# Triangular inverse of a gated delta-rule layer: two matmul levels and a Newton step are replaced by a VectorE level, one float32 level and a substitution

## The chip, the cores and the metric

The kernel runs on one core of a Trainium2 chip. The metric is the device time of one execution in microseconds. The core has five engines with an instruction queue each, all in order: TensorE (PE), VectorE (DVE), ScalarE (ACT), GpSimd (POOL), and SyncE (SP), which here only waits on semaphores and issues DMAs.

## The reference

One layer on x of 2 x 2048 tokens by 256 features. The attention part is a gated delta rule with 8 key heads and 16 value heads of 128 x 128 state:

```python
mixed = silu(causal_conv4(layernorm(x) @ Wqkv.T + bqkv))   # q, k (8 heads), v (16 heads)
beta, g = sigmoid(x @ Wb.T + bb), -exp(A_log) * softplus(x @ Wa.T + ba + dt_bias)
def step(state, (q_t, k_t, v_t, g_t, b_t)):                # for each token, each head
    state = state * exp(g_t)
    delta = (v_t - k_t @ state) * b_t
    state = state + outer(k_t, delta)
    return state, q_t @ state
core = rmsnorm(outs) * norm_w * silu(x @ Wz.T + bz)
x = x + layernorm(core @ Wout.T + bout)
x = x + layernorm(shared_ffn(h) + top8_of_16_experts(h))   # h = layernorm(x)
```

## The kernel before

The tokens are cut into 32 chunks of 128. Inside a chunk the recurrence is a linear system: with the strictly lower triangular 128 x 128 matrix L of each head (decayed products of keys), delta = (I + L)^-1 (...). The kernel builds the inverse explicitly, then solves with a matmul. The 16 heads go in 4 groups of 4, and one pass of the software pipeline, an *item*, is one group of one chunk: 128 items, and each engine's queue is written out by hand in its own `item` function. In item w several groups are at work: a = w+3 (projection and convolution), f = w+2 (keys, decays, L), v = w+1 (merging of the inverse), w itself (state and output), and the feed-forward part of the chunk before.

The inverse of group f takes this road. POOL writes minus L (`minus_l`, L1484). SP writes it to DRAM (`triangle_out`, L408, tensor DL), and reads back the eight 16 x 16 diagonal blocks of each of the 4 heads as 32 lanes of 256 numbers (`blocks_in`, L412, tile Cb). POOL inverts them by doubling, 22 instructions that each wait for the one before, and turns the result (`base_inverse`, L1583 to L1607, tile Yb). SP writes block inverses and their transposes to DRAM (`inverses_out`, L417, DX), waits until they have landed and reads them as 128 x 128 matrices (`inverses_in`, L424 and L425, tiles XiT and Xi). Then come three merging levels on TensorE in float32r (`invert_q` L547, `invert_xt` L560, `invert_x` L570), each with a mask on DVE (`mask_q`, L1194) and PSUM copies on ACT (L937, L944), and a Newton step (`turned`, `residual`, `correct`; L577, L584, L586, L593) that ends in the copy to Tt (`refined`, L1210). The state part of item w (`ks_qs`, `solve`, `az`, `new_state`) uses Tt in two halves of two heads.

In SP's item the order is: Xf of the next chunk, Xr of this one (in one item of four each), then `triangle_out(f)`, `blocks_in(f)`, `inverses_out(f)`, `inverses_in(f)`, and the store of the chunk. So SP issues 6 DMAs in an item, and 3 more per chunk.

Of the kernel before, what the change touches and what calls it, by code (L numbers as in the profile page):

```python
# [33 lines left out]
F32R = mybir.dt.float32r  # L34
# [5 lines left out]
P = 128  # L40
# [5 lines left out]
GK = HK // GROUPS  # L46
TILES = 2 * GK + GH
TAPS = 4
LO = 4
LEVELS = 7 - LO  # L50
SLOTS = 8
BASE = 1 << LO
BLOCKS = P // BASE
LANES = BLOCKS * GH
HSTRIDE = P * P + P
# [11 lines left out]
C_KEEP = C_LEVEL + LEVELS * P  # L67


def constants(chunks, chunks_of_batch):  # L70
# [8 lines left out]
    for n in range(LEVELS):  # L79
        b = r >> (LO + n)  # L80
        f[:, C_LEVEL + n * P:C_LEVEL + (n + 1) * P] = (b[:, None] % 2 == 1) & (b[None, :] == b[:, None] - 1)
    f[:, C_LEVEL:C_LEVEL + P] += np.eye(P)
# [19 lines left out]
def layer_kernel(nc, x, wqkv, conv, wz, wba, rows, cols, wout, shared1, wlat, shared2, wup, rw, rw2,  # L102
# [6 lines left out]
    with ctx:  # L109
# [22 lines left out]
        IdR = sb("IdR", [P, GH, P], F32R)  # L132
        NegR = sb("NegR", [P, P], F32R)
# [35 lines left out]
        Vs = sb("Vs", [P, GROUPS, GH, P])  # L169
        Kn = sb("Kn", [P, GROUPS, GK, P])  # L170
        AT = sb("AT", [P, GROUPS, GH, P])
# [13 lines left out]
        Ln = sb("Ln", [P, 2, GH, P])  # L185
        LnR = sb("LnR", [P, GH, P], F32R)


        Xi = sb("Xi", [P, GH, P], F32R)
        XiT = sb("XiT", [P, GH, P], F32R)  # L190
        Qi = sb("Qi", [P, GH, P], F32R)
# [4 lines left out]
        Yb = sb("Yb", [LANES, 2, BASE * BASE], F32R)  # L196
        Tp = sb("Tp", [LANES, BASE ** 3 // 8])
        Tm = sb("Tm", [LANES, BASE * BASE // 4])
        DL = nc.dram_tensor("DL", (GH * HSTRIDE,), F32, kind="Internal").ap()
# [9 lines left out]
        def blocks_of(part):  # L209
            return scratch(part, [[BASE * (P + 1), LANES], [P, BASE], [1, BASE]])  # L210
# [6 lines left out]
        Z = sb("Z", [P, 2, P])  # L217
        O = sb("O", [P, GH, P])
# [27 lines left out]
        def heads(bank):  # L246
# [3 lines left out]
        BASE_STEPS = 2 + sum(2 * (3 if n == 1 else BASE // (2 << n) + n) for n in range(1, LO))  # L250
# [3 lines left out]
            q_full=LEVELS + 1, xt_full=LEVELS, x_full=LEVELS - 1, xr_full=1, c_full=1,  # L254
            ks_full=2, qs_full=2, zs_full=2, az_full=2, ds_full=2, coT_full=1, po_full=1,

            y_done=2, silu_done=2, gz_done=1, zb_done=1, lnk_done=1, rki_done=1, sc_done=1, partsT_done=1, ex_done=1,
            kn_done=1, vs_done=1, xi_done=LEVELS, qg_done=2, z_done=2, lnf_done=1, fr_done=1, coT_done=1,
            xt_done=LEVELS, sq_done=1, lnr_done=1, oq_done=1,

            bk_done=1, tails_done=2, convqk_done=TAPS, convv_done=TAPS, sse_done=1, epq_done=1, kkq_done=1, hg_done=4, parts_done=5,
            q_done=LEVELS + 1, tt_done=1, r_done=2, o_done=2, s_done=2, so_done=1, vv_done=1, core_done=1, acc_done=1,
# [3 lines left out]
            ln_out=16, lc_in=16, xs_out=32, xs_seen=1, xb_in=32,  # L266
# [34 lines left out]

        def ahead(w, n):

            t, g = w
            return t + (g + n) // GROUPS, (g + n) % GROUPS

        def run(eng, item):
# [6 lines left out]
            steps = next(n for n in (30, 6, 5, 3, 2, 1) if (chunks - 2) % n == 0)  # L314
            with eng.Fori(0, (chunks - 2) // steps) as i:
                for k in range(steps):
                    for g in range(GROUPS):
                        item((i * steps + k + 1, g), "cafispe")
# [57 lines left out]
        def _(sp):  # L376
# [29 lines left out]
            def triangle_out(f):  # L406
                sp.wait_ge(sem["neg_done"], at("neg_done", f))
                sp.dma_start(rows_of(DL), Ln[:, f[1] % 2, :, :]).then_inc(sem["ln_out"], 16)  # L408

            def blocks_in(f):  # L410
                sp.wait_ge(sem["ln_out"], at("ln_out", f))
                sp.dma_start(Cb[:, :].rearrange("p (i j) -> p i j", i=BASE), blocks_of(DL)).then_inc(sem["lc_in"], 16)  # L412

            def inverses_out(f):
                sp.wait_ge(sem["base_done"], at("base_done", f))
                for n in range(2):
                    sp.dma_start(blocks_of(DX[n]), Yb[:, n, :].bitcast(F32).rearrange("p (i j) -> p i j", i=BASE))\  # L417
                        .then_inc(sem["xs_out"], 16)

            def inverses_in(f):  # L420
                sp.wait_ge(sem["xs_out"], at("xs_out", f))
                sp.sem_inc(sem["xs_seen"], 1)
                sp.wait_ge(sem["c_full"], at("c_full", ahead(f, -1)))
                sp.dma_start(XiT[:, :, :].bitcast(F32), rows_of(DX[1])).then_inc(sem["xb_in"], 16)  # L424
                sp.dma_start(Xi[:, :, :].bitcast(F32), rows_of(DX[0])).then_inc(sem["xb_in"], 16)  # L425

            def item(w, stages):
                t, g = w
                f = ahead(w, 2)
# [17 lines left out]
            run(sp, item)  # L447
# [4 lines left out]
        def _(pe):  # L452
# [45 lines left out]
            def ss(f):  # L498
                pe.wait_ge(sem["xt_done"], at("xt_done", ahead(f, -2)))
# [17 lines left out]
            def vtr(f):  # L517
                pe.wait_ge(sem["tt_done"], at("tt_done", ahead(f, -2)))
# [15 lines left out]
            def invert_q(v, n, front=None):  # L534
                if n == 0:
                    if front:
                        pe.wait_ge(sem["ex_done"], at("ex_done", ahead(v, 1)))
                    else:
                        pe.wait_ge(sem["q_done"], at("q_done", ahead(v, -1)))
                    pe.wait_ge(sem["xb_in"], at("xb_in", v))  # L540
                    mm(bQ[:, :], identb, identb.unsqueeze(1).to_broadcast([P, GH, P]), start=True, stop=True)
                    pe.wait_ge(sem["lnr_done"], at("lnr_done", v))
                else:
                    pe.wait_ge(sem["xt_done"], at("xt_done", v, n))
                    pe.wait_ge(sem["q_done"], at("q_done", v, n))
                for h in range(GH):
                    last = mm(heads(bQ)[:, h, :], LnR[:, h, :], XiT[:, h, :], start=(n > 0), stop=True,  # L547
                                  skip_group_check=True)
                last.then_inc(sem["q_full"], 1)

            def invert_xt(v, n, front=None):
                if n == 0 and front:
                    pe.wait_ge(sem["partsT_done"], at("partsT_done", ahead(v, 1)))
                elif n == 0:
                    pe.wait_ge(sem["xt_done"], at("xt_done", ahead(v, -1)))
                pe.wait_ge(sem["q_done"], at("q_done", v, n + 1))
                if n:
                    pe.wait_ge(sem["xi_done"], at("xi_done", v, n))
                for h in range(GH):
                    last = mm(heads(bXT)[:, h, :], Xi[:, h, :], Qi[:, h, :], start=(n == 0 and h == 0), stop=True,  # L560
                              skip_group_check=True)
                last.then_inc(sem["xt_full"], 1)

            def invert_x(v, n, front=None):
                if n == 0 and front:
                    pe.wait_ge(sem["vs_done"], at("vs_done", ahead(v, 1)))
                elif n == 0:
                    pe.wait_ge(sem["tt_done"], at("tt_done", ahead(v, -1)))
                for h in range(GH):
                    last = mm(heads(bX)[:, h, :], Qi[:, h, :], Xi[:, h, :], start=(n == 0 and h == 0), stop=True,  # L570
                                  skip_group_check=True)
                last.then_inc(sem["x_full"], 1)

            def turned(v):
                pe.wait_ge(sem["xt_done"], at("xt_done", v))
                for h in range(GH):
                    last = mm(heads(bX)[:, h, :], XiT[:, h, :], IdR[:, 0, :], start=(h == 0), stop=True, skip_group_check=True)  # L577
                last.then_inc(sem["xr_full"], 1)

            def residual(v):  # L580
                g = v[1]
                pe.wait_ge(sem["neg_done"], at("neg_done", v))
                for h in range(GH):
                    mm(heads(bQ)[:, h, :], Ln[:, g % 2, h, :], XiT[:, h, :].bitcast(F32), start=(h == 0), stop=False,  # L584
                       skip_group_check=True)
                mm(bQ[:, :], NegR[:, :], XiT[:, :, :], start=False, stop=True, skip_group_check=True)\  # L586
                    .then_inc(sem["q_full"], 1)

            def correct(v):
                pe.wait_ge(sem["xi_done"], at("xi_done", v))  # L590
                pe.wait_ge(sem["q_done"], at("q_done", v))
# [1089 lines left out]
```

## Time and profile before

| | |
|---|---|
| median of 3 runs | 3363.12 us (3360.05 to 3366.53) |
| profiled execution, first to last instruction | 3361.6 us |
| TensorE busy | 3184.6 us, 95% |
| VectorE / ScalarE / GpSimd busy | 2731.3 / 2411.1 / 2147.3 us |
| mean granted TensorE clock | 0.989 |

The profiled execution's own time is not listed apart from its span; the span is 1.5 us under the median of the runs. Busy times are sums over instructions. A matmul's end is modelled and overlaps the next one, so that the spacing of starts, not the duration, tells what a matmul costs. A float32 matmul is two records in the trace.

### The profile page before, as it was taken

The numbers are of one execution on the slowest core, as the hardware profiler recorded it, in microseconds if no ns is written. First come the engines' busy times: TensorE is split into PE (matmuls) and PEld (weight loads), VectorE is DVE, ScalarE is ACT, GpSimd is POOL, SyncE is SP. The second block draws the span as 40 slices with busy tenths as digits, with TensorE's granted clock in tenths as the row PEclk, the third lists the DMA queues.
The fourth block names the chain that finished last, engine by engine and source line by source line (L and its number), as shares of the span: only waits on it lengthen the run. The fifth ranks groups of instructions, "written<-read, shape, count | busy, mean of one in ns | idle before, by whom it ended". The sixth has DMA issues, their size and how long they took to land.

```text
span 3361.6 us, 77100 instructions
## 1 busy us (share of the span) xinstructions
PE 3184.6 (95%) x23968; PEld 2828.4 (84%) x23968; DVE 2731.3 (81%) x8720; ACT 2411.1 (72%) x5922; POOL 2147.3 (64%) x5380
## 2 busy tenths in 40 slices
PE   4999999999999999999999999999999999999996
PEld 3888888888888888888888888888888888888885
DVE  4788888888888888888888888888888888888874
ACT  3777777777777777777777777777777777777762
POOL 3766666666666666666666666666666666666660
PEclk8999999999999999999999999999999999999997
DMA  4111111111111111111111111111111111111110
GB/s 182 43 40 38 44 40 35 45 41 38 39 45 35 39 47 38 36 45 38 38 45 41 36 37 46 38 39 47 37 35 45 41 38 42 43 35 39 47 36 11
DMA packets 424113, 144.75 MB, mean 43 GB/s; under 512 B 211168, under 2 KB 421664, under 8 KB 423200
## 3 DMA queue, kind: packets, MB, share of 16 engines
q1 hardware_dynamic: 423712, 139.83, 15.9%
q8 instruction: 200, 3.28, 0.4%
q14 instruction: 201, 1.65, 0.2%
HBM read 93.11 MB, written 46.66 MB: 42 GB/s over the span
## 4 chain that ended last, share of the span: by engine, by line
PE 66%; ACT 14%; DVE 5%; issue 5%; POOL 5%; DMA 4%; SPq 0%; ACTq 0%; DVEq 0%; POOLq 0%
PE bF L474 8%; PE bB L648 6%; PE bQ L547 5%; ACT L850 4%; PE bXT L560 4%; PE bB L733 3%; PE bB L720 3%; PE bS L615 3%; PE bD L630 3%; PE bS L623 3%; PE bF L485 3%; PE bS L607 3%; PE bF L487 3%; PE bD L608 2%; PE bX L570 2%
## 5 line engine op out<-in xcount | busy, mean ns | idle before, releaser
L1151 DVE SCALAR_TENSOR_TENSOR Y<-bF,Cv,Y 128x127 f32<-128x127 f32 (+2 forms) x3072 | 852.2, 339 | 8.3 <-ACT Y L867 3.4
L474 PE MATMUL bF<-XnT,Wqkv 128*128 128x128 f32 x4096 | 530.9, 277 | 0.5 <-ACT XnT L986 0.5
L474 PEld LDWEIGHTS bF<-XnT,Wqkv 128*128 128x128 f32 x4096 | 504.4, 193 | 9.3 <-issue 1.8
L867 ACT ACTIVATE Y<-bF,Cv 128x128 f32<-128x128 f32 x1024 | 383.4, 455 | 102.5 <-PE bF L474 102.5
L937 ACT ACTIVATE XiT<-bXT 128x512 fp32r<-128x512 f32 x384 | 229.0, 596 | 298.0 <-PE bXT L560 293.4
L1590 POOL TENSOR_TENSOR Tp<-Tp 32x64 f32<-32x64 f32 (+2 forms) x768 | 362.1, 472 | 60.2
L1194 DVE TENSOR_TENSOR Qi<-bQ,Cf 128x512 fp32r<-128x512 f32 x384 | 262.8, 684 | 98.1 <-PE bQ L547 97.0
L850 ACT ACT_TABLE_LOAD x257 | 329.7, 1283 | 5.4 <-PEq L1674 0.7
L560 PEld LDWEIGHTS bXT<-Qi,Xi 128*128 128x128 f32 x1536 | 221.8, 191 | 118.0 <-issue 88.8
L560 PE MATMUL bXT<-Qi,Xi 128*128 128x128 f32 x1536 | 298.7, 317 | 14.3 <-DVE Qi L1194 2.5
L1583 POOL TENSOR_TENSOR Tp<-Yb,Tm 32x64 f32<-32x64 f32 (+1 forms) x384 | 276.0, 719 | 30.1
L1583 POOL TENSOR_TENSOR Tp<-Cb,Yb 32x64 f32<-32x64 f32 (+1 forms) x384 | 274.6, 715 | 30.1
L1598 POOL TENSOR_TENSOR Yb<-Cb,Cf 32x8 fp32r<-32x8 f32 x128 | 25.9, 202 | 402.1 <-DMA Cb<-DL 402.1
L547 PE MATMUL bQ<-XiT,LnR 128*128 128x128 f32 x1536 | 264.2, 295 | 19.6 <-ACT XiT L937 19.5
L547 PEld LDWEIGHTS bQ<-XiT,LnR 128*128 128x128 f32 x1536 | 211.6, 191 | 41.1 <-ACT XiT L937 29.1
L648 PE MATMUL bB<-Wout,CoT 128*128 128x256 f32 x1024 | 244.2, 382 | 0.9 <-ACT CoT L973 0.8
L1484 POOL TENSOR_TENSOR Ln<-Ex,KKQ 128x512 f32<-128x512 f32 x128 | 163.1, 1274 | 125.6 <-issue 121.7
L944 ACT ACTIVATE Xi<-bX 128x512 fp32r<-128x512 f32 x384 | 228.4, 595 | 3.6 <-PE bX L577 2.3
L1517 POOL TENSOR_TENSOR HG<-LnbG,Lnk 128x4 f32<-128x4 f32 x128 | 29.2, 228 | 295.5 <-ACT Lnk L900 295.4
L648 PEld LDWEIGHTS bB<-Wout,CoT 128*128 128x128 f32 x1024 | 185.9, 192 | 21.6 <-ACT CoT L973 1.2
L615 PE MATMUL bS<-R,Tt 128*128 128x128 f32 x1024 | 165.9, 285 | 9.9 <-DVE Tt L1210 9.9
L1020 ACT ACTIVATE Rl<-bB 128x512 f32<-128x512 f32 x124 | 74.1, 597 | 139.0 <-PE bF L721 139.0
(234 smaller groups left out, 9269.8 us busy)
## 6 DMA issues: line engine op xcount, KB each, us to landing
DL<-Ln SPq DMA_DIRECT2D x128, 256.0 KB, 2.2
XiT<-DX SPq DMA_DIRECT2D x128, 256.0 KB, 2.8
Xi<-DX SPq DMA_DIRECT2D x128, 256.0 KB, 3.2
DX<-Yb SPq DMA_DIRECT2D x256, 32.0 KB, 1.9
Xf<-x SPq DMA_DIRECT2D x32, 128.0 KB, 3.1
Wqkv<-wqkv SPq DMA_DIRECT2D x4, 1024.0 KB, 17.0
Cb<-DL SPq DMA_DIRECT2D x128, 32.0 KB, 1.9
Xr<-x SPq DMA_DIRECT2D x32, 128.0 KB, 3.3
```

Source lines behind the costliest of these rows:

```text
L474: last = mm(bank[:, i, :], Wqkv[:, k, c:c + P], XnT[:, k, :], start=(k == 0), stop=(k == KT - 1))
L547: last = mm(heads(bQ)[:, h, :], LnR[:, h, :], XiT[:, h, :], start=(n > 0), stop=True, skip_group_check=True)
L560: last = mm(heads(bXT)[:, h, :], Xi[:, h, :], Qi[:, h, :], start=(n == 0 and h == 0), stop=True, skip_group_check=True)
L615: last = mm(heads(bS)[:, i, :], Tt[:, 2 * p + i, :], R[:, i, :], start=True, stop=True)
L648: last = mm(bB[:, 0:HID], CoT[:, h, :], Wout[:, g * GH + h, :], start=(h == 0), stop=(h == GH - 1))
L850: nc.scalar.add_instruction(mybir.InstLoadActFuncSet(name=nc.get_next_instruction_name(), act_func_set_id=TABLES[name], engine=mybir.Engin ...
L867: last = op(Y[:, tile, :], bank[:, i, :], ACT.Identity, scale=c[:, TAPS - 1:TAPS], bias=c[:, TAPS:TAPS + 1])
L937: op(XiT[:, :, :], heads(bXT), ACT.Copy).then_inc(sem["xt_done"], 1)
L1151: last = stt(y, bank[:, i, 0:P - shift], Cv[:, g * TILES + tile, n:n + 1], y, ALU.mult, ALU.add)
L1194: tt(Qi[:, :, :], heads(bQ), level, ALU.mult).then_inc(sem["q_done"], 1)
L1583: then(tt(view(Tp[:, :], p * m ** 3, [[m * m, m], [m, m], [1, m]]), pair(left, p), pair(right, p), ALU.mult))
L1590: then(tt(lo, lo, hi, ALU.add))
```

## The change

Of the 128 x 128 inverse only the two 64 x 64 diagonal halves are built. The doubling on POOL to 16 x 16 blocks stays, with the same instructions and sizes, but is cut in two: the steps of width 1, 2 and 4 for f in item w, the last step (width 8) for v at the start of the next item, and the turning late in that item. Level 16 to 32 goes to DVE, on 128 lanes of 2 rows (`wide`, 5 instructions). Level 32 to 64 is one float32 level on TensorE (`merge_q`, `mask_q`, `merge_x`) with one addition on DVE (`merged`). The last level is never formed: the solve becomes a substitution (`solve_halves`, `solve_cross`, `solve_rest`) with two ACT copies of 64 rows (`upper_half`, `crossed`). The Newton step and its identities go. Tiles Vs, Kn, AT and Ln become rings of three, Yb is doubled.

The DVE level needs its operands on other lanes, and this is done by DMAs of 16 partitions. SP's new functions and its order:

```diff
+            def cross_in(f):
+                sp.wait_ge(sem["wide_done"], at("wide_done", ahead(f, -1)))
+                for n in range(SPREAD):                      # SPREAD = 8
+                    sp.dma_start(Cm[n * PAIRS:(n + 1) * PAIRS, :]..., blocks_of(DL, 0, BASE)).then_inc(sem["cm_in"], 16)
+            def inverses_spread(v):
+                sp.wait_ge(sem["base_done"], at("base_done", v, BASE_STEPS - 1))
+                sp.wait_ge(sem["wide_done"], at("wide_done", ahead(v, -1)))
+                for n in range(SPREAD):
+                    sp.dma_start(Ya[n * PAIRS:(n + 1) * PAIRS, :], Yb[0:PAIRS, ...]).then_inc(sem["ya_in"], 16)
+                for n in range(SPREAD):
+                    sp.dma_start(Yc[n * PAIRS:(n + 1) * PAIRS, :], Yb[PAIRS:LANES, ...]).then_inc(sem["yc_in"], 16)
+            def crosses_out(v):
+                sp.wait_ge(sem["wide_done"], at("wide_done", v))
+                for n in range(SPREAD):
+                    sp.dma_start(rows_in_blocks(DX[0], ..., ROWS_OF, BASE), Yu[...]).then_inc(sem["xu_out"], 16)
+                    sp.dma_start(rows_in_blocks(DX[1], ..., BASE, ROWS_OF), Yv[...]).then_inc(sem["xv_out"], 16)
...
+                if "i" in stages:
+                    inverses_spread(v)
+                if "f" in stages:
+                    triangle_out(f)
                 if g == 1 and "s" in stages:
                     tokens_in(t)
+                if "i" in stages:
+                    inverses_out(v)                          # 4 DMAs, waits for the turning
+                    crosses_out(v)
                 if "f" in stages:
-                    triangle_out(f)
                     blocks_in(f)                             # 2 DMAs instead of 1
-                    inverses_out(f)
-                    inverses_in(f)
+                if "i" in stages:
+                    inverses_in(v)                           # waits for xs_out, xu_out, xv_out
+                if "f" in stages:
+                    cross_in(f)
```

The DVE level, and POOL's new order:

```diff
+            def wide(v):
+                dve.wait_ge(sem["cm_in"], at("cm_in", v))
+                dve.wait_ge(sem["ya_in"], at("ya_in", v))
+                tt(terms, across(Ya), down(Cm), ALU.mult)            # 128 x 512
+                nc.vector.tensor_reduce(Tr, summed, AX.X, ALU.add)   # 128 x 32 <- 128 x 512
+                dve.wait_ge(sem["yc_in"], at("yc_in", v))
+                tt(terms, across(Tr), down(Yc), ALU.mult)            # 128 x 512
+                nc.vector.tensor_reduce(Yu, summed, AX.X, ALU.add)
+                nc.vector.tensor_copy(Yv, Yu turned)                 # 128 x 32
...
 POOL item:
+  base_terms(v,3,0) base_halved(v,3,0,0) exponents(f) base_halved(v,3,0,1) base_joined(v,3,0) base_terms(v,3,1)
+  edge_terms(a) base_halved(v,3,1,0) base_halved(v,3,1,1) key_exponents(f) base_joined(v,3,1)
+  edge_sum(a,0) exponent_part/rest(f,0) edge_sum(a,1) exponent_part/rest(f,1) exponent_part(f,2)
+  decay_keys(w,0) minus_l(f) attention(f) base_turned(v) decay_keys(w,1)
+  base_ones(f) end_exponents(f) base_terms/halved/joined(f,1..2)
```

TensorE's merging and solve, and the masks:

```diff
-   invert_q x3, invert_xt x3, invert_x x2, turned, residual, correct, solve
+   merge_q(v):       mm(bQ[h], Ln[ring(v), h], XiT[h])            # 4 x float32
+   merge_x(w):       mm(bX[h], Qi[h], Xi[h])                      # 4 x float32, early in the next item
+   solve_halves(w,p) mm(bS[i], Tt, R)  -> ACT upper_half (64 rows of Ym)
+   solve_cross(w,p)  mm(bX[..], Ln, Ym) -> ACT crossed (64 rows of Wm)
+   solve_rest(w,p)   mm(bS[i], Tt, Wm), added in PSUM
-   DVE: mask_q x4, refined (copy)      ACT: inverse_t x3, inverse x3, rounded_l
+   DVE: mask_q x1, merged (addition)   ACT: upper_half x2, crossed x2
```

All five queues are put into a new order. On DVE `wide(v)` stands after `update_o(w, 0)` and ahead of `right_side(w, 1)`; on TensorE `merge_q(v)` is nearly the last step of the item and `merge_x` the third of the next; `update_s(w, 1)` is DVE's last. Masks, norms and sums stay on the engines they are on.

## Rows read from the trace of the kernel before

**Rows 1.** The page: busy time of each engine, and TensorE's granted clock in 40 slices.
```profile
PE 3184.6 (95%) x23968; PEld 2828.4 (84%) x23968; DVE 2731.3 (81%) x8720; ACT 2411.1 (72%) x5922; POOL 2147.3 (64%) x5380
PEclk8999999999999999999999999999999999999997
```

**Rows 2.** Busy time by stretch, from the first to the last issue of Cb.
```profile
53.20:3269.30 3216.10, 3102.80 (x23438) 2759.33 (x23438) 2662.42 (x8516) 2364.32 (x5813) 2128.19 (x5327) 1.00 0.16 40
```

**Rows 3.** The chain of waits, one stretch: start, us, what, records.
```profile
1610.54 0.89 PE bF L474 x8
...
1613.03 0.45 PE bS L623 x4
...
1614.81 0.21 PE bQ L541
1615.03 0.40 PE bQ L547 x4
...
1616.47 0.65 PE bXT L560 x4
```

**Rows 4.** Groups of instructions by shape, DVE and ACT: busy us, mean ns.
```profile
L1194 DVE TENSOR_TENSOR Qi<-bQ,Cf 128x512 fp32r<-128x512 f32 x384 | 262.8, 684 | 98.1 <-PE bQ L547 97.0
L937 ACT ACTIVATE XiT<-bXT 128x512 fp32r<-128x512 f32 x384 | 229.0, 596 | 298.0 <-PE bXT L560 293.4
L956 ACT ACTIVATE Z<-bS 128x256 f32<-128x256 f32 x256 | 102.2, 399 | 19.3 <-PE bS L615 19.3
L1210 DVE COPY Tt<-bX 128x512 f32<-128x512 f32 x128 | 88.4, 690 | 6.4 <-PE bX L593 3.0
L1240 DVE TENSOR_REDUCE Ss<-CoT 128x4 f32<-128x512 f32 x128 | 86.0, 672 | 0.0
L1157 DVE TENSOR_SCALAR Bk<-Cv,Cf 128x8 f32<-128x8 f32 x128 | 29.2, 228 | 0.0
```

**Rows 5.** SP's DMA issues in order of time: start us, us, instruction.
```profile
1606.26 0.85 SPq L417 DMA_DIRECT2D DX<-Yb  x2
1608.58 0.38 SPq L424 DMA_DIRECT2D XiT<-DX  x1
1609.00 0.51 SPq L425 DMA_DIRECT2D Xi<-DX  x1
1609.55 0.50 SPq L404 DMA_DIRECT2D out<-Yo  x1
1610.10 0.43 SPq L400 DMA_DIRECT2D Xf<-x  x1
1615.28 0.37 SPq L408 DMA_DIRECT2D DL<-Ln  x1
1617.46 0.32 SPq L412 DMA_DIRECT2D Cb<-DL  x1
```

**Rows 6.** One line of the kernel: duration of each issue of DX (ns).
```profile
L417 SPq DMA_DIRECT2D DX<-Yb x256: 303/321/1230, 67.3 to 3283.8; - x128
```

**Rows 7.** The page: DMA issues, KB each, median us to landing; queue's packets.
```profile
Xi<-DX SPq DMA_DIRECT2D x128, 256.0 KB, 3.2
DX<-Yb SPq DMA_DIRECT2D x256, 32.0 KB, 1.9
Cb<-DL SPq DMA_DIRECT2D x128, 32.0 KB, 1.9
q1 hardware_dynamic: 423712, 139.83, 15.9%
```

**Rows 8.** Waits, SP's queue and POOL: us in total, times, longest.
```profile
SPq L417 <- POOL Yb L1607: 1797.1, 128, 15.1
POOL Yb L1598 <- DMA Cb<-DL: 402.1, 128, 4.7
```

**Rows 9.** POOL in order of time, one item: start us, us, instruction.
```profile
1609.16 0.20 POOL L1517 TENSOR_TENSOR HG<-LnbG,Lnk 128x4 f32<-128x4 f32 x1 [2.62 <-ACT Lnk L900]
...
1610.90 0.23 POOL L1498 TENSOR_TENSOR Hd<-Tails,Cv 128x24 f32<-128x24 f32 x1
...
1615.21 1.26 POOL L1484 TENSOR_TENSOR AT<-Ex,KKQ 128x512 f32<-128x512 f32 x1
1619.40 0.20 POOL L1598 TENSOR_TENSOR Yb<-Cb,Cf 32x8 fp32r<-32x8 f32 x1 [2.92 <-DMA Cb<-DL]
...
1630.55 0.29 POOL L1592 TENSOR_TENSOR Yb<-Tp 32x64 fp32r<-32x64 f32 x1
1630.91 0.72 POOL L1607 TENSOR_TENSOR Yb<-Yb,Cf 32x256 fp32r<-32x256 f32 x1
```

More of the change, by code:

```diff
@@ L305, in ahead, with run @@
             return t + (g + n) // GROUPS, (g + n) % GROUPS
-        def run(eng, item):
+        def run(item):
             for g in range(GROUPS):
@@ L313, in run @@
                 item((0, g), "cafis" + "p" * (g > 0))
[L314 to L318, printed above, removed]
+            for t in range(1, chunks - 1):
+                for g in range(GROUPS):
+                    item((t, g), "cafispe")
             for g in range(GROUPS):
@@ L414, in inverses_out @@
-            def inverses_out(f):
-                sp.wait_ge(sem["base_done"], at("base_done", f))
                 for n in range(2):
[L417 to L425, printed above, removed]
+                    sp.dma_start(Cb[n * PAIRS:(n + 1) * PAIRS, :].rearrange("p (i j) -> p i j", i=BASE),
+                                 blocks_of(DL, n * BASE, n * BASE)).then_inc(sem["lc_in"], 16)
@@ new lines, in inverses_out @@
+            def inverses_out(v):
+                sp.wait_ge(sem["base_done"], at("base_done", v))
+                sp.wait_ge(sem["xb_in"], at("xb_in", ahead(v, -1)))
+                for n in range(2):
+                    for half in range(2):
+                        sp.dma_start(blocks_of(DX[n], half * BASE, half * BASE),
+                                     Yb[half * PAIRS:(half + 1) * PAIRS, v[1] % 2, n, :].rearrange("p (i j) -> p i j", i=BASE))\
+                            .then_inc(sem["xs_out"], 16)
@@ L446, in _ @@
             sp.wait_ge(cleared, 32)
-            run(sp, item)
+            run(item)
             sp.wait_ge(stored, 16 * (chunks + 1))
@@ L564, in invert_x @@
[L564 to L571, printed above, removed]
-                last.then_inc(sem["x_full"], 1)
@@ L574, in turned @@
[L574 to L587, printed above, removed]
@@ L614, in solve, with solve_cross, solve_rest @@
                 for i in range(2):
-                    last = mm(heads(bS)[:, i, :], Tt[:, 2 * p + i, :], R[:, i, :], start=True, stop=True)
+                    last = mm(heads(bS)[:, i, :], Tt[:, 2 * p + i, :], R[:, i, :], start=(i == 0), stop=False,
+                              skip_group_check=True)
+                last.then_inc(sem["ys_full"], 1)
+            def solve_cross(w, p, front):
+                t, g = w
+                pe.wait_ge(sem["ym_done"], at("ym_done", w, p + 1))
+                if p == 1 and front:
+                    pe.wait_ge(sem["vs_done"], at("vs_done", ahead(w, 2)))
+                for i in range(2):
+                    last = mm(heads(bX)[:, 2 * p + i, :], Ln[:, ring(w), 2 * p + i, :], Ym[:, i, :], start=True, stop=True)
+                last.then_inc(sem["ws_full"], 1)
+            def solve_rest(w, p):
+                t, g = w
+                pe.wait_ge(sem["wv_done"], at("wv_done", w, p + 1))
+                for i in range(2):
+                    last = mm(heads(bS)[:, i, :], Tt[:, 2 * p + i, :], Wm[:, i, :], start=False, stop=True,
+                              skip_group_check=True)
                 last.then_inc(sem["zs_full"], 1)
@@ L840, in _ @@
             pe.wait_ge(early, 16 * len(EARLY))
-            run(pe, item)
+            run(item)
         @block.scalar
@@ L1469, in item @@
                     experts(t - 1, "result", 0)
+                if invert:
+                    mask_q(v)
+                if state:
+                    out_norm(w)
                 if c and g == 0:
                     chunk_front(t + 1, "ba")
-            run(dve, item)
+                if state:
+                    update_s(w, 1)
+            run(item)
         @block.gpsimd
@@ new lines, in base_halved, with base_joined @@
+            def base_halved(f, n, side, k):
+                m, pairs, left, right, into = operands(f, n, side)
+                width = m >> (k + 1)
+                base_wait(f, base_steps(n, side) + terms_of(n) + k)
+                lo = view(Tp[:, :], 0, [[m, pairs * m * m], [1, width]])
+                hi = view(Tp[:, :], width, [[m, pairs * m * m], [1, width]])
+                tt(lo, lo, hi, ALU.add).then_inc(sem["base_done"], 1)
+            def base_joined(f, n, side):
+                m, pairs, left, right, into = operands(f, n, side)
+                base_wait(f, base_steps(n, side) + terms_of(n) + n - 1)
+                if m == 2:
+                    halves = [view(Tp[:, :], k * 4 * pairs, [[4, pairs], [2, 2], [1, 2]]) for k in range(2)]
+                else:
+                    halves = [view(Tp[:, :], k, [[m ** 3, pairs], [m * m, m], [m, m]]) for k in range(2)]
+                tt(into, halves[0], halves[1], ALU.add).then_inc(sem["base_done"], 1)
@@ L1614, in item @@
                 new, front, invert, state, post, e, c = [s in stages for s in "afispec"]
+                if invert:
+                    base_terms(v, 3, 0)
+                    base_halved(v, 3, 0, 0)
                 if front:
                     exponents(f)
+                if invert:
+                    base_halved(v, 3, 0, 1)
+                    base_joined(v, 3, 0)
+                    base_terms(v, 3, 1)
                 if new:
[L1618 removed]
+                    edge_terms(a)
+                if invert:
+                    base_halved(v, 3, 1, 0)
+                    base_halved(v, 3, 1, 1)
+                if front:
+                    key_exponents(f)
+                if invert:
+                    base_joined(v, 3, 1)
+                if new:
+                    edge_sum(a, 0)
+                if front:
+                    exponent_part(f, 0)
+                    exponent_rest(f, 0)
+                if new:
+                    edge_sum(a, 1)
+                if front:
+                    exponent_part(f, 1)
+                    exponent_rest(f, 1)
+                    exponent_part(f, 2)
                 if state:
[L1620 removed]
+                    decay_keys(w, 0)
                 if front:
@@ L1623, in item @@
                     attention(f)
-                    base_inverse(f)
-            run(pool, item)
+                if invert:
+                    base_turned(v)
+                if state:
+                    decay_keys(w, 1)
+                if front:
+                    base_ones(f)
+                    end_exponents(f)
+                    base_terms(f, 1, 0)
+                    base_joined(f, 1, 0)
+                    base_terms(f, 1, 1)
+                    base_joined(f, 1, 1)
+                    base_terms(f, 2, 0)
+                    base_halved(f, 2, 0, 0)
+                    base_joined(f, 2, 0)
+                    base_terms(f, 2, 1)
+                    base_halved(f, 2, 1, 0)
+                    base_joined(f, 2, 1)
+            run(item)
 def kernel(**inputs):
```

632 lines of the change are left out of this document (316 added, 316 removed).

## The prediction

> **What bounds the kernel now.** I read the page first: TensorE is busy 95% of the span at a granted clock of 1.00 in all but the outermost slices, VectorE 81%, the others less [rows 1]. Then the stretch from the first to the last issue of Cb, which is 127 items: 3216.1 / 127 = 25.32 us an item, of which TensorE is busy 24.4, VectorE 21.0, ScalarE 18.6 and GpSimd 16.8 [rows 2]. The rest of the span, 3361.6 - 3216.1 = 145.5 us, is ramp. So TensorE's queue sets the pace, and an edit counts there first. Then the transfers: SP issues few and waits long, 1797 us in all for the block inverses (14 us of every item), and GpSimd waits 402 us (3.1 us an item) for Cb [rows 8]. These waits cost nothing today, because the inverse is made an item ahead. The reader should keep the roles in mind: before, SP is idle most of an item.
>
> **What the change takes off and puts on the engines, per item.** TensorE: a float32 matmul of 128 columns costs 0.22 us (four in 0.89, two in 0.45); four float32r ones cost 0.40 to 0.65 us, I take 0.5 [rows 3]. Removed are 40 float32r matmuls (3+3+2+1+1 groups of four: 10 x 0.5 = 5.0), four float32 (0.9), a bf16 identity of 512 columns (0.21) and a float32r one, bounded by 0.2 and 0.9, taken as 0.3: 6.4 us. Added are merge_q, merge_x, solve_cross and solve_rest, 4 float32 each: 16 x 0.22 = 3.6 us. Net -2.8 us. VectorE: three masks of 0.684 go (-2.05); the copy to Tt at 0.690 becomes an addition of the same size, taken equal. `wide` is two products of 128x512 and two reductions of 128x512, nearest rows 0.684 and 0.672, and a copy of 32 columns, between 0.2 and 0.7 (I take 0.2): 2.9 us. Net +0.9, so 21.9 us [rows 4]. ScalarE loses seven copies of 0.6 and gains four of 64 rows by 256, at most 0.4 each by the row of Z, at least nothing: -2.6 to -4.2. GpSimd keeps its instructions. If engines alone counted, TensorE's item would be 25.3 - 2.8 = 22.5 us.
>
> **What it does to the queue of SP.** Transfers per item: `inverses_spread` 16, `triangle_out` 1, `inverses_out` 4, `crosses_out` 16, `blocks_in` 2, `inverses_in` 2, `cross_in` 8: 49 where there were 6. Every issue occupies SP. The shortest of 256 issues of DX lasts 303 ns [rows 6]; in a burst the starts stand 0.42 to 0.55 us apart, and the pair for DX takes 0.85 us [rows 5]. Size hardly matters in these rows: 32 KB in 0.32, 256 KB in 0.37 to 0.51. No row shows an issue of 16 partitions. The new transfers leave in bursts of 8 and 16, so the nearest row is the pair: i = 0.85 / 2 = 0.425 us each. The low end is 0.30, the high end 0.55 (the longest spacing in these rows). A cost below 0.30 is no end of this range; it is the rival below.
>
> 49 x 0.425 = 20.8 us of issuing would still fit into an item. What does not fit is that most of it has become serial with GpSimd. SP's order puts `blocks_in(f)` behind `crosses_out(v)`, and the group f of this item is the v of the next. The circle, starting when GpSimd has joined the last block of v:
>
> 1. 16 spreads; the last begins after 15 i and lands 1.9 us later [rows 7]. The landing of a transfer inside SBUF is not shown; I take that of Cb and DX.
> 2. `wide` can do its first two instructions before Yc is there, but product, reduction and turning come after: 0.68 + 0.67 + 0.2 = 1.6 us [rows 4].
> 3. `crosses_out` waits for this. 16 issues, then the two of Cb, the last of which begins after 17 i and lands after 1.9 us.
> 4. GpSimd waits for Cb and doubles. Today the 22 steps from L1598 to the last L1592 take from 1619.40 to 1630.84, 11.4 us [rows 9]. The same steps, in the same sizes, with about seven small instructions set between them (exponents, edge_terms, key_exponents, end_exponents, at 0.2 each, some in today's gaps), are 12.6 us. They end in the join that starts the next circle.
>
> Sum: 32 i + 1.9 + 1.6 + 1.9 + 12.6 = 32 i + 18.0. With i = 0.425 it is 31.6 us an item, against 22.5 that TensorE would need. It is equal to today's 25.3 at i = 0.23.
>
> Other edits are hidden in this circle. The 4 issues of `inverses_out` and the one of DL lie between the spread and the landing of Yc plus `wide` (5 i = 2.1 against 1.9 + 1.6), unless the turning is late: after the join come the parts, decay_keys, minus_l, attention and the turning, by today's rows 7.3 us from L1517 to the end of attention with 0.6 for the edge terms and 0.6 for the second decay_keys to be taken off, and 0.7 for the turning, 6.8 in all; the spread takes 16 i = 6.8. So it is covered at 0.425 and decides only for small i. `inverses_in` and `cross_in` (10 i, and the landing of Yv) fall beside GpSimd's 12.6 us. A second circle goes through TensorE: join, spread, wide (15 i + 3.5), 16 crosses and their landing (15 i + 1.9), XiT and Xi (i + 3.2), merge_q 0.9, mask 0.7, then in the next item merge_x 0.9, ss 0.9, proj 0.9, kkq 0.9, the halves and qs 0.9, ScalarE's Qg and Ln 0.9, key_exponents and the join 0.6: 31 i + 16.2 = 29.4 us. It is 2 us under the first, so TensorE waits but does not add. On VectorE, `wide` waits in front of `right_side(w, 1)`, the second taps and `update_s`: all of this stands still until Yc has landed, and TensorE with it; their work after the wait is some 10 us and has room in 31.6.
>
> The 64-byte and 8-byte rows of Cm and Yv bring the packets from 3310 an item to some 7900 (Cm 2048, Yv 2048, Yu 256, Ya and Yc 256). The queue's packets take 15.9% of 16 engines now, 20 ns each [rows 7]. At that mean a Yv transfer keeps its 16 engines 0.32 us, less than one issue; I count nothing. At twice the mean it would be 0.64 and the eight would add 1.7 us an item, 220 us, which is inside my range.
>
> Sum for the run: 127 x 31.6 = 4013, and the ramps unchanged at 145.5: a span of 4159 us. Runs lie 1.5 us over the span before, so 4160 us.
>
> **A rule of the skill against this.** The shortest issue in this trace is 303 ns [rows 6]. The Trainium skill (DMA: Bandwidth & Descriptors, Anatomy of one DMA) puts the sequencer's dispatch of one DMA at about 50 ns and calls descriptor generation small; it describes GpSimd's path. The trace disagrees sixfold for SP. With 0.05 and the 0.04 us that stand between two issues, i = 0.09, the change would be a gain, as follows.
>
> **The rivals.** *B, cheap small issues (faster).* An issue of 16 partitions might cost much less than one of 32 or 128. The mechanism decides at i = 0.23. Under it the first circle falls behind another: join to turning 6.8, then 4 + 16 + 2 issues, landing 1.9, GpSimd 12.6: 21.3 + 22 i. At i = 0.09 that is 23.3 us, over TensorE's 22.5 and VectorE's 21.9: 127 x 23.3 + 145.5 = 3105 us. For it: no row has this shape, and cost varies a little with shape. Against: seven forms of transfers between 32 KB and 256 KB in this stretch all lie at 0.32 or above [rows 5]. 0.12.
>
> *C, TensorE loses its clock, or bursts jam (far slower).* TensorE's work would be 21.6 us of a 31.6 us item, with its idle time in one piece in front of `right_side(w, 1)`. The granted clock is below 1.00 only in the first and last slices, where it idled [rows 1]. At the lower of its two levels, 1.2 for 2.4 GHz, all of its work would take 43 us and the run over 5600; with a third of the work at that level it takes 29 us and stays hidden. Bursts at 0.55 us give 35.6 us an item, 4670 us. What lies beyond 4640: 0.06.
>
> *D, no change in time.* The circle might be looser than I read it and end near 25.3 by chance: 3360 us, 0.02. That the engines' own work becomes the bound is excluded, none grows by more than 0.9 us.
>
> **How the numbers follow.** Forecast 0.80, B 0.12, C 0.06, D 0.02. A measurement of this kernel tells 0.2% (7 us) from no change. i = 0.30 gives 27.6 us and 3650 us, 0.55 gives 4670; the range is 3610 to 4640, which leaves out B, C and D. Since nearly all of the chance has one sign, this is the forecast's own range too. Faster 0.12, same 0.02, slower 0.86.
>
> **What would show it.** Issues of Cb some 31.6 us apart; 16 issues of Ya and Yc in about 6.8 us; VectorE idle before the second product of `wide` for Yc, GpSimd idle before L1598's successor for Cb, longer than 3.1 us an item; TensorE busy near 70%. Wrong would be: issues of 16 partitions under 0.23 us, or Cb issued before the crosses are out, or TensorE idle for something else than VectorE's queue.

## The result, and the profile after

The changed kernel takes 4850.0 us (median of 4 runs, 4846.7 to 4854.0), the kernel before 3362.1 us beside it: 1.442 times as long, 95% interval 1.440 to 1.444. The direction was forecast, the size was not: 4160 us were forecast, and the time lies 210 us over the upper end of the range.

The page of the changed kernel, busy time and granted clock [rows 1]:

```profile
PE 3353.3 (69%) x21664; PEld 2860.1 (59%) x21664; DVE 3106.5 (64%) x8976; ACT 2178.7 (45%) x5538; POOL 2175.1 (45%) x5380
PEclk7888889888888888888888898888888888888887
```

No engine is busy 70% of the span any more, and the granted clock has fallen from 0.99 to 0.86 of 2.4 GHz. The chain that ended last, by engine and by line, from the same page:

```profile
SPq 44%; POOL 28%; DMA 10%; issue 10%; DVE 5%; PE 1%; POOLq 0%; ACT 0%; DVEq 0%; ACTq 0%
SPq L451 13%; POOL Tp L1644 11%; SPq L453 11%; SPq L468 10%; SPq L470 9%; POOL Tp L1653 7%; DMA Cb<-DL 5%; DMA Yc<-Yb 5%; DVE Tq L1230 3%; POOL Tp L1640 2%; POOL Yb L1662 2%; POOL Tm L1662 2%; DVE Yu L1233 2%; SPq L437 1%; POOL Hd L1537 1%
```

TensorE, 95% busy before, is on 1% of this chain. SP's queue, which does nothing but issue DMAs, is on 44% of it, GpSimd on 28%, landings on 10%. One turn of the chain, in order of time (start us, us, what), is the circle of the prediction:

```profile
2429.01 0.52 SPq L451
2429.57 0.62 SPq L451
...
2434.24 0.58 SPq L453
...
2438.02 0.59 SPq L453
2438.65 1.84 DMA Yc<-Yb
2440.59 1.03 DVE Tq L1230
2441.64 0.70 DVE Yu L1233
2442.57 0.30 SPq L468
2442.91 0.42 SPq L470
...
2447.69 1.66 SPq L470
...
2451.32 0.45 SPq L437
2451.81 1.88 DMA Cb<-DL
...
2458.30 1.48 POOL Tp L1644
...
2465.01 1.20 issue
2466.71 0.52 SPq L451
```

L451 and L453 are the 16 spreads (9.6 us from the first to the start of the last, which is not on a line of its own: its landing is counted from there), then Yc lands, VectorE finishes `wide`, L468 and L470 are the 16 crosses (8.7 us), L437 the two reads of Cb, then GpSimd's doubling up to the next spread. This turn is 2466.71 - 2429.01 = 37.7 us. Over the run the issues of Cb span 55.3 to 4741.4 us, 36.9 us an item where it was 25.3 [rows 2], and 159 us are ramp. The waits (us in total, times, longest) that answer to those of before [rows 8]:

```profile
POOL Yb L1623 <- DMA Cb<-DL: 1909.0, 128, 17.1
PE bS L635 <- DVE R L1258: 962.2, 127, 9.6
DVE Tq L1230 <- DMA Yc<-Yb: 389.5, 128, 4.1
SPq L451 <- POOL Yb L1662: 1039.3, 128, 11.5
POOL HG L1559 <- ACT Lnk L933: 141.2, 79, 8.7
```

GpSimd waits 14.9 us of each item for Cb, where it was 3.1; TensorE waits 7.5 us for the right side that stands behind `wide` in VectorE's queue. The durations of single issues in ns (shortest, median, longest), to set beside [rows 6]:

```profile
L451 SPq DMA_DIRECT2D Ya<-Yb x1024: 507/589/1836, 69.5 to 4758.6; - x171
L468 SPq DMA_DIRECT2D DX<-Yu x1024: 302/448/1832, 82.9 to 4774.4; - x171
L470 SPq DMA_DIRECT2D DX<-Yv x1024: 302/423/1827, 83.3 to 4774.9; - x171
L443 SPq DMA_DIRECT2D Cm<-DL x1024: 303/448/1560, 56.2 to 4746.7; - x171
```

Here is the largest mis-sized term: a transfer from 16 partitions to 16 others (2 KB for Ya, and 16 KB for Yc with the same median) holds SP for 0.59 us. No transfer of the kernel before went from SBUF to SBUF, and the longest median of its transfers inside an item was 0.51 us.

### The profile page after: what moved, and what is told of

Same layout as the page of the kernel before. It is cut to its first block, busy times and chain, and to the rows that moved or that the text cites. A ratio compares the mean times of both kernels' runs of the same rounds, so it can differ in the third digit from the quotient of the medians.

```text
span 4844.9 us, 78493 instructions
## 1 busy us (share of the span) xinstructions
PE 3353.3 (69%) x21664; PEld 2860.1 (59%) x21664; DVE 3106.5 (64%) x8976; ACT 2178.7 (45%) x5538; POOL 2175.1 (45%) x5380
## 3 DMA queue, kind: packets, MB, share of 16 engines
q1 hardware_dynamic: 1101600, 179.90, 19.8%
q14 instruction: 250, 2.05, 0.1%
## 4 chain that ended last, share of the span: by engine, by line
SPq 44%; POOL 28%; DMA 10%; issue 10%; DVE 5%; PE 1%; POOLq 0%; ACT 0%; DVEq 0%; ACTq 0%
SPq L451 13%; POOL Tp L1644 11%; SPq L453 11%; SPq L468 10%; SPq L470 9%; POOL Tp L1653 7%; DMA Cb<-DL 5%; DMA Yc<-Yb 5%; DVE Tq L1230 3%; POOL Tp L1640 2%; POOL Yb L1662 2%; POOL Tm L1662 2%; DVE Yu L1233 2%; SPq L437 1%; POOL Hd L1537 1%
## 5 line engine op out<-in xcount | busy, mean ns | idle before, releaser
L635 PEld LDWEIGHTS bS<-R,Tt 128*128 128x128 f32 x1024 | 197.7, 260 | 995.3 <-issue 979.9
L965 ACT ACTIVATE Ym<-bS 64x256 f32<-64x256 f32 x256 | 96.4, 377 | 1036.6 <-PE bS L635 1036.6
L1230 DVE TENSOR_TENSOR Tq<-Tr,Yc 128x512 f32<-128x512 f32 x128 | 130.2, 1018 | 389.5 <-DMA Yc<-Yb 389.5
L1225 DVE TENSOR_TENSOR Tq<-Ya,Cm 128x512 f32<-128x512 f32 x128 | 175.9, 1374 | 310.5 <-DMA Ya<-Yb 310.5
L1267 DVE TENSOR_TENSOR O<-Qg,bS 128x256 f32<-128x256 f32 x256 | 107.8, 421 | 372.5 <-ACT Qg L976 349.3
L686 PE MATMUL bB<-Wout,CoT 128*128 128x256 f32 x1024 | 339.8, 492 | 0.8 <-ACT CoT L998 0.8
L668 PEld LDWEIGHTS bD<-Z,Kd 128*128 128x128 f32 x1024 | 196.0, 264 | 213.9 <-issue 212.1
L668 PE MATMUL bD<-Z,Kd 128*128 128x128 f32 x1024 | 223.0, 358 | 137.5 <-ACT Qg L976 137.5
L686 PEld LDWEIGHTS bB<-Wout,CoT 128*128 128x128 f32 x1024 | 266.5, 275 | 46.8 <-ACT CoT L998 1.1
L1275 DVE SCALAR_TENSOR_TENSOR S<-S,Sc,bD 128x128 f32<-128x128 f32 x512 | 153.9, 341 | 149.6 <-PE bD L668 149.6
```

Source lines behind the costliest of these rows:

```text
L635: last = mm(heads(bS)[:, i, :], Tt[:, 2 * p + i, :], R[:, i, :], start=(i == 0), stop=False, skip_group_check=True)
L668: last = mm(heads(bD)[:, i, :], Kd[:, p, i, :], Z[:, i, :], start=True, stop=True)
L686: last = mm(bB[:, 0:HID], CoT[:, h, :], Wout[:, g * GH + h, :], start=(h == 0), stop=(h == GH - 1))
```

## The experiments

The theory is the circle through SP. Its rivals: the clock, the engine work of the new design, the total of issuing or of packets, and a second circle that was underrated. The runs on the changed kernel are medians of two executions, those on the kernel before of four.

### How much of the loss is the issues

All five families of eight DMAs cut to one each, with otherwise the same queues:

```diff
-  cm_in=16 * SPREAD, ya_in=16 * SPREAD, yc_in=16 * SPREAD, xu_out=16 * SPREAD, xv_out=16 * SPREAD
+  cm_in=16, ya_in=16, yc_in=16, xu_out=16, xv_out=16
-                for n in range(SPREAD):      # in cross_in, inverses_spread (twice), crosses_out
+                for n in range(1):
```

> Each of the five families of eight DMAs (Ya, Yc, Yu, Yv, Cm) is cut to its first one: 14 issues an item instead of 49. Seven eighths of the lanes are left unmoved (zeros), so the output is not the reference's; every engine instruction stays. Theory (the circle through SP): the issues leave it and what is left runs over the turning: join to turning 7.1 us, 4 + 2 + 2 issues at 0.47, landing 1.9, GpSimd 12.6 = 25.4 us an item, 3390 us, and the granted clock of TensorE back near 1.0. Rival (the new DVE level, the substitution and the new queue order are slow by themselves, or the clock does it): stays above 4400.

Measured: 3669.5 us, ratio 1.091 (1.086 to 1.096). The 35 issues, with what they move, are 1181 of the 1488 us that the change costs. The granted clock is back at 0.944 with nothing changed but these transfers, so most of its fall was a consequence. The time is not 3390, because the chain has moved to VectorE (40%) and TensorE (33%); 306 us over the kernel before remain.

### Which issues

Only Ya and Yc cut to one:

> Only Ya and Yc are cut to one DMA each (left unmoved lanes are zeros, so the output is not the reference's). Theory: 14 issues of 0.65 us leave the circle, 9.1 us, but the turning then decides (7.1 us after the join): 7.1 + 20 issues x 0.48 + 2 x 0.47 + 1.9 + 12.6 = 32.2 us an item, 4240 us. Rival (all issues cost the same 0.425 us, and the excess over the forecast is something else, such as the clock): 14 x 0.425 = 6 us off, 31 us an item or 4090, with the spacing of Ya at 0.42.

Measured: 4538.8 us, 300 us over the theory's figure. The removal of 9 us of issues brought 2.4 us an item. The turning decides as expected (SP waits 267 us for it and 555 us for minus L), but the way to it does not lead over GpSimd's doubling, as the figure had it. The chain of this run goes from Cb's landing over two small steps of GpSimd and ScalarE's Qg into TensorE's queue, and from there to minus L, the masked attention (AT), the turning and the crosses. TensorE is on 34% of it, SP's queue on 26%.

Only Yu and Yv cut to one:

> Only Yu and Yv are cut to one DMA each (the rest of the cross blocks stays zero, so the output is not the reference's). Theory: 14 issues of 0.48 us leave the circle: 36.9 - 6.7 = 30.2 us an item, 3990 us. Rival (the small rows of 8 and 64 bytes jam the DMA engines, and the issues only queue up behind them): more than that, since 2048 of 8600 packets go, and the spacing of the Ya issues falls under 0.6.

Measured: 4491.8 us, 500 us over. Spacing of the Ya issues is still 0.63 us, so that no jam behind small rows is what makes them long. What took over is in its waits:

```profile
POOL HG L1559 <- ACT Lnk L933: 695.8, 127, 8.5
```

That is 5.5 us an item, where it was 1.1 with all the crosses. L1559 is key_exponents, which stands just before the join. Lnk comes from ScalarE, behind Qg, behind TensorE's next item: the second circle, which the prediction put 2 us under the first.

Only Cm cut to one:

> Only Cm is cut to one DMA (the rest of the lanes are zeros, so the output is not the reference's). Theory: these issues stand beside GpSimd's doubling and are not on the circle: no change, 4850 within 30 us. Rivals: SP's total issuing time is the bound, then 7 x 0.49 = 3.4 us an item go, 4410 us; or the number of packets is, then more.

Measured: 4841.6 us, against 4850.0: no change. 896 issues and 229 thousand packets less bring nothing, because they stand where SP waits anyway: its wait for the join grows from 1039 us in all to 1378. Neither the total of issuing nor the number of packets is the bound.

### The second circle

SP's reads of Cb ahead of the writes:

```diff
+                if "f" in stages:
+                    blocks_in(f)
                 if "i" in stages:
                     inverses_out(v)
                     crosses_out(v)
-                if "f" in stages:
-                    blocks_in(f)
```

> One reordering of SP: the reads of Cb go ahead of the writes of the block inverses and of the crosses. One-circle theory (only spread, wide, crosses, Cb, doubling counts, as forecast): 16 x 0.63 + 0.53 + 2.3 for DL to land + 0.95 + 1.9 + 12.6 = 28.4 us an item, 3770 us. Two-circle theory (the way over XiT, merge_q, Qg, Ln and key_exponents back to the join is as long, 37 us): SP now also waits for DL to land ahead of the crosses, so 37.4 + 2.3 = 39.7 us an item, 5200 us.

Measured: 5164.0 us, as the theory of two circles had it (5200) and far from 3770. From the chain of this run (start us, us, what) and its waits:

```profile
2402.07 2.33 DMA DL<-Ln
2404.42 0.32 SPq L437
2404.79 1.89 DMA Cb<-DL
...
2417.87 15.20 issue
2433.10 0.20 POOL HG L1559
```

```profile
POOL HG L1559 <- ACT Lnk L933: 1605.5, 127, 15.2
POOL Yb L1623 <- DMA Cb<-DL: 844.3, 128, 8.6
```

GpSimd now has Cb early, has done everything up to key_exponents by 2417.9, and stands 15.2 us for Lnk (the wait is on its line in the second block; the chain calls it issue). The first circle is cut, and the second is longer by the 2.3 us of DL's landing.

The same, with the second circle cut as well:

```diff
+                if invert:
+                    base_joined(v, 3, 1)
                 if front:
                     key_exponents(f)
-                if invert:
-                    base_joined(v, 3, 1)
```

> The same reordering, and on GpSimd key_exponents moves behind the join, so that the join no longer waits for TensorE's next item. Two-circle theory: the second circle is cut; what is left goes from wide over crosses, XiT, merge_q and VectorE's queue to the next wide: 13.7 + 2.3 + 13.5 + 3.9 = 33.4 us an item, 4410 us. If SP's total issuing were the bound (26.5 us and its waits of 4): 30.5 us, 4040.

Measured: 4512.3 us, 2% over the 4410 of the theory and 650 us under the run before it. Moving one 0.2 us instruction of GpSimd by one place is worth 5.1 us an item there. The same move with SP's order left as it was in the changed kernel was not run.

### Why a spread costs 0.63 us

Ya and Yc in the same shapes, from DRAM:

```diff
-  sp.dma_start(Ya[...], Yb[0:PAIRS, v[1] % 2, 0, n * k:(n + 1) * k])
+  sp.dma_start(Ya[...], bass.AP(DZ.tensor, DZ.offset + n * k, [[BASE * BASE, PAIRS], [1, k]]))
-  sp.dma_start(Yc[...], Yb[PAIRS:LANES, v[1] % 2, 0, :])
+  sp.dma_start(Yc[...], bass.AP(DZ.tensor, DZ.offset, [[BASE * BASE, PAIRS], [1, BASE * BASE]]))
```

> Ya and Yc are read in the same 16-partition shapes, but from a DRAM scratch of zeros instead of Yb (so the output is not the reference's). Theory A (the source or the way inside SBUF makes these issues long): spacing falls from 0.63 to the 0.49 of Cm, 16 x 0.14 = 2.2 us an item, 4570 us. Theory B (the shape, one short row for each DMA engine, makes it): spacing stays 0.63 and the time 4850.

Measured: 4570.6 us, where theory A had 4570. The row of L454 in this run:

```profile
L454 SPq DMA_DIRECT2D Yc<-DZ x1024: 302/420/2027, 71.5 to 4492.3; - x171
```

0.42 us instead of 0.59, for the same 16 rows of 1 KB. Reading SBUF alone does not make an issue long (Yu and Yv to DRAM: 0.45 and 0.42), nor does writing it (Cm from DRAM: 0.45). So it is the way from SBUF to SBUF that does, not the size or the shape. Why, no run shows. That the time hit 4570 is partly chance: the spacing fell further than the theory had it, from 0.63 to 0.46 us, which is 2.7 us for 16, and 2.2 us an item came of it.

### What is left without the issues

The run with one DMA of each family, and the products and reductions of `wide` on 64 instead of 512 numbers a lane:

```diff
-  terms = lanes(Tq[:, :], [[BASE * BASE, ROWS_OF], [BASE, BASE], [1, BASE]])
+  terms = lanes(Tq[:, :], [[BASE * BASE, 1], [BASE, 4], [1, BASE]])
```

> As the run with one DMA of each family, and the products and reductions of the DVE level cut from 512 to 64 numbers a lane (most of the level is left out, so the output is not the reference's). Theory (with the issues gone, VectorE's queue with wide in its middle is the bound; wide takes 3.9 us instead of 2.9, and it slows GpSimd beside it): 3 us an item less than 27.7, 3290 us. Rival (order of TensorE's queue and its hops over ScalarE in the substitution): 3670 stays.

Measured: 3477.7 us, 192 us under the run with the full width, half of what was expected. By form, from the run at full width (busy us, mean ns):

```profile
L1228 DVE TENSOR_TENSOR Tq<-Ya,Cm 128x512 f32<-128x512 f32 x128 | 132.3, 1033 | 0.5 <-DMA Ya<-Yb 0.5
L1233 DVE TENSOR_TENSOR Tq<-Tr,Yc 128x512 f32<-128x512 f32 x128 | 168.3, 1315 | 4.5
L1239 DVE COPY Yv<-Yu 128x32 f32<-128x32 f32 x128 | 53.2, 415 | 4.5
L1524 POOL TENSOR_TENSOR AT<-Ex,KKQ 128x512 f32<-128x512 f32 x128 | 262.6, 2052 | 0.0
```

and from the run with the narrow level:

```profile
L1235 DVE TENSOR_TENSOR Tq<-Tr,Yc 128x64 f32<-128x64 f32 x128 | 57.2, 447 | 4.6 <-DVE Tr L1232 0.2
L1241 DVE COPY Yv<-Yu 128x32 f32<-128x32 f32 x128 | 119.3, 932 | 4.6 <-DVE Yu L1238 0.2
L1526 POOL TENSOR_TENSOR AT<-Ex,KKQ 128x512 f32<-128x512 f32 x128 | 163.2, 1275 | 0.0
```

The products take 1.0 to 1.3 us where 0.68 was forecast, and while they run GpSimd's product AT, the masked attention, takes 2.05 us; with narrow products it takes 1.28, as in the kernel before. Two things are in these figures. One is the product's own cost, which the changed kernel shows, where GpSimd stands idle for Cb during the second product of every turn:

```profile
L1230 DVE TENSOR_TENSOR Tq<-Tr,Yc 128x512 f32<-128x512 f32 x128 | 130.2, 1018 | 389.5 <-DMA Yc<-Yb 389.5
```

It takes 1015 to 1020 ns in all 128 turns, with nothing beside it. That both inputs are in SBUF does not explain this by itself: in the same run a sum of two SBUF tiles of 128x256 in plain order (X<-X,Xr) takes 432 ns, and one with an input in PSUM (Acc<-bB,Rows) 425. What the products have besides is one input read in steps of 16 numbers and one read repeatedly; no run separates these. The other thing is the two engines in each other's way: beside AT the second product takes 1.3 instead of 1.02 us and AT 2.05 instead of 1.27. The copy of 32 columns, 0.18 us in the changed kernel with GpSimd idle, takes 0.42 us here, and 0.93 us with the narrow level, so that a part of this only moves. The Trainium skill (SBUF — State Buffer, Who interferes with whom) says that a VectorE instruction with two inputs in SBUF contends with a GpSimd instruction that reads SBUF; the rows of the products and of AT agree. The products have both inputs in SBUF, the masks that they replace had one in PSUM.

The run stays 111 us over the 3366.6 us of the kernel before beside it. These are open: the substitution's hops over ScalarE and the order of TensorE's queue were not tried by themselves.

### The part of the change that pays

In the kernel before, only the Newton step taken out (the inverse is then as exact as float32r makes it):

```diff
-                if state:
-                    correct(w)
...
-                    invert_xt(v, 2)
+                    invert_x(v, 2)          # waits for q_done and xi_done; bX is then the inverse
...
-                    turned(v)
-                    residual(v)
...
-                    inverse_t(v, 2)         # ScalarE
-                    inverse(v, 2)           # ScalarE
-                    mask_q(v, 3)            # VectorE
```

> The kernel before with one part of the change alone: the Newton step goes (turned, residual, correct, its mask and two PSUM copies), the third float32r level ends directly in Tt; the levels, SP's six DMAs and all other orders stay. The inverse is then as exact as float32r makes it. Theory (TensorE's queue is the bound of the kernel before): 12 float32r and 4 float32 matmuls, one of 512 columns and one transposed set less, 2.2 us an item: 3363 - 127 x 2.2 = 3085 us, 3250 at most if hops between engines take half of it back. Rival (TensorE only looks busy, the hops over ScalarE and VectorE are the bound): 3360.

Measured: 3299.0 us, ratio 0.982 (0.980 to 0.984). It beats both kernels, the one before by 1.8%. But 62 us are 0.5 us an item, of an estimated 2.2 us that left TensorE's queue. (The expectation's count of 12 float32r matmuls leaves out that four come in for them: the records fall by 17 an item, which is 8 float32r, 4 float32 of two records and the one of 512 columns, and these give the 2.2 us. The busy time of TensorE fell by 1.5 us an item.) Its page and its chain:

```profile
PE 2992.6 (91%) x21792; PEld 2598.3 (79%) x21792; DVE 2660.8 (81%) x8592; ACT 2272.7 (69%) x5666; POOL 2153.2 (65%) x5380
PE 49%; POOL 18%; issue 9%; ACT 9%; DMA 7%; DVE 7%; SPq 0%; POOLq 0%; ACTq 0%; DVEq 0%
```

A TensorE that was busy 95% had other chains close behind it: GpSimd with the DMA landings, those of DL and Cb above all, is now on a quarter of the chain (it was 9%).

To shorten that chain, two steps of GpSimd were put ahead of its wait for Lnk, with the Newton step out and with it in:

```diff
+                if new:
+                    before_first(a)
+                if state:
+                    decay_keys(w)
                 if front:
                     exponents(f)
-                if new:
-                    before_first(a)
-                if state:
-                    decay_keys(w)
```

> The kernel before without its Newton step, and on GpSimd before_first(a) and decay_keys(w) go ahead of exponents(f), into the wait for Lnk (1.8 us an item in the run without the Newton step) and off the way from the keys to minus L. Theory (without the Newton step the circle through GpSimd, DL and Cb has become the bound, 18% of the chain of waits is GpSimd's there): 0.7 to 1.5 us an item less than 3299, 3110 to 3210 us. Rival (TensorE and its hops are still the bound): 3299 stays, or some more where exponents now come later.

> The kernel before with only that reordering of GpSimd; the Newton step stays. Theory: TensorE's queue is the bound of the kernel before, so nothing to gain: 3360 within 15 us. Rival (GpSimd's circle is the second bound already): some 60 us less.

Measured: 3460.8 us (1.028 of the kernel before, 1.025 to 1.031) and 3421.7 us (1.016, 1.014 to 1.018). Both theories missed: the reordering is slower both times, by 162 us against the run without the Newton step and by 57 us. The rival of the first had named the cause (exponents come later), though not the size. The waits of the first run:

```profile
POOL Ln L1451 <- ACT Ex L904: 455.8, 128, 5.5
PEld bXT L515 <- issue: 142.7, 45, 6.6
PE bXT L515 <- POOL Parts L1497: 135.1, 45, 6.5
```

Without the reordering the wait before Ln was 124.5 us in all, here it is 455.8. The exponent parts come later, TensorE waits for them in the middle of its queue (L515), and the decays (Ex) with everything behind come later too. GpSimd's wait for Lnk was not free time for its neighbours.

## Why the prediction was wrong, point by point

The circle's terms in us, as forecast, in the turn shown, and as the mean of 126 turns of the run, taken from the starts of the same instructions:

| term | forecast | turn shown | mean |
|---|---|---|---|
| first spread to the start of the last, 15 i | 6.4 | 9.6 | 9.6 |
| Yc lands, VectorE starts | 1.9 | 1.9 | 1.9 |
| `wide` after Yc | 1.6 | 2.0 | 2.0 |
| first cross to the start of the last Cb, 17 i | 7.2 | 9.2 | 8.5 |
| Cb lands, GpSimd starts | 1.9 | 1.9 | 2.0 |
| GpSimd to the next spread | 12.6 | 13.0 | 12.9 |
| sum | 31.6 | 37.7 | 36.9 |

**What bounds the kernel before: half right.** TensorE's queue is the first bound, but not with 2.8 us of room under it. Removing an estimated 2.2 us gave 0.5. The 22.5 us an item and with it rival B's 3105 us were too low: even with nearly all the new issues gone the item is 27.7 us.

**The circle: right.** Its stations and order are those of the chain shown above, Cb is issued behind the crosses, `inverses_out` and DL hide in front of `wide`, Cm hides (4841.6 against 4850.0).

**The issue cost i: the step that failed.** It was 0.425 for all. The spreads cost 0.64 us each with the gap: 3.3 us an item more. The crosses and Cb cost 0.47 to 0.49 from start to start, plus single issues of 1.2 to 2.1 us in some items, as in the turn shown: 9.24 us from the first cross to the last Cb for the 17 x 0.425 = 7.2, 2.0 more, of which 1.2 are that one issue; in the mean it is 1.2 more. The spreads alone would have given 34.9 us an item, near 4580 us, which is inside the range; the crosses, `wide` and the wait at the end took it out. The upper end of the range took 0.55 from bursts of large transfers; no row of before was a transfer inside SBUF, and the text said so of its landing but not of its issue. In the mean i is (9.6 + 8.5) / 32 = 0.57. The range ended at 4640, though its own upper end of i gives 4670.

**`wide`: too cheap.** From Yc's landing to the first cross it takes 2442.57 - 2440.59 = 2.0 us against 1.6, because the product takes 1.02 us and not 0.68, with no instruction of GpSimd beside it. The first product, which is not in this term, takes 1.37 us in the mean, some of it beside GpSimd.

**GpSimd's part: right in its sum.** 2466.71 - 2453.75 = 13.0 us against 12.6, with 1.2 of it spent waiting for Lnk. So the work itself was 0.8 us shorter than forecast, and a wait that the forecast put at nothing made up for it, by luck. Landings were 1.84 and 1.88 against 1.9.

**The packets.** Some 7900 an item were forecast; the queue moved 1101600 in all, 8606 an item:

```profile
q1 hardware_dynamic: 1101600, 179.90, 19.8%
```

Their time is 14 ns each by this row, not the 20 of before, and counting nothing for them was right: 229 thousand fewer changed nothing in the run with one Cm.

**The second circle: underrated.** It was put at 29.4 us, 2 under the first, and lies within some 1 us of it: the join waits for Lnk in 79 of its turns, 141.2 us in all, 1.1 us an item. The same spreads are in it, and the granted clock of TensorE's part is 0.86. In the changed kernel it adds about this wait and little more. But it meant that no single cut of the first circle could give its full value (4539 and 4492 us where 4240 and 3990 were expected).

**The clock: a consequence.** It was 0.862 with the issues and 0.944 without most of them, and TensorE is on 1% of the chain that the clock would have to lengthen. Rival C, with a chance of 0.06 for all beyond 4640, is where the time fell: not by its clock, but by its other half, bursts with a spacing over 0.55 us.

**TensorE busy near 70%: true by luck.** It is 69%, but as 26.2 us of work at a lower clock in an item of 36.9 us, not as 21.6 us in 31.6.

**Rival B, cheap small issues: wrong.** A transfer of 16 partitions costs SP no less than one of 32 or 128; the shortest of 1024 crosses is 302 ns, where it was 303 before. The 50 ns for a dispatch that the Trainium skill gives (DMA: Bandwidth & Descriptors, Anatomy of one DMA) stand there for GpSimd's path; no issue of SP's queue in any run here is near them.

## What to carry to other kernels

Count the DMAs that an edit adds on the queue that issues them, at the spacing that the runs here show: 0.42 to 0.49 us from start to start between 2 KB and 256 KB, and 0.63 from SBUF to SBUF; then look for a circle in which a wait of that queue stands behind a burst. A transfer that only rearranges lanes costs as many issues as it has pieces, and here 32 of them outweighed an estimated 2.8 us of matmuls. Look for the second circle before cutting the first: with the reads of Cb moved up, a 0.2 us instruction that stood one place too early cost 5.1 us an item. And where a row is borrowed for an instruction that reads in other steps, widen its price: the product took 1.02 us where a mask of the same size took 0.68.

## What was unexpected of the hardware

- The same transfer of 16 rows of 1 KB occupies SP for 0.59 us from SBUF and 0.42 us from DRAM.
- Single issues last up to 2.1 us among others of 0.45, some of them in the middle of a burst; the cause is open.
- A product of 128x512 on VectorE with one input read in steps of 16 numbers took 1.02 us with GpSimd idle, where masks of 128x512 took 0.68.
- With products on VectorE whose inputs are both in SBUF, a 128x512 product on GpSimd beside them went from 1.27 to 2.05 us, and the product on VectorE from 1.02 to 1.3.
- A copy of 32 columns on VectorE took 0.18 us with GpSimd idle, 0.42 and 0.93 us beside GpSimd's products.
